# Third layer of a four-layer network on one Trainium2 core: VectorE's scans, statistics and last additions moved behind the multiplications of the first gates, denominators' sums one gate sooner

## The chip, the cores and the metric

The kernel runs on one core of a Trainium2 chip, in one launch. The metric is device time in microseconds. TensorE (PE) does the matrix products, VectorE (DVE), ScalarE (ACT) and GpSimd (POOL) the rest, SyncE (SP) issues the DMAs. Each engine has its own queue and works it off in order. An instruction that waits for a semaphore holds up all that stands behind it on its engine.

## The reference

Four layers run one after the other on x of 4 × 512 × 256 floats. Each is `x = x + attention(layernorm(x)) + feedforward(layernorm(x))`. The change touches only the third:

```
# attention: linear, with a decayed running sum over the tokens
q, k, v = split(xn @ w_qkv);  q, k = elu(q) + 1, elu(k) + 1      # 16 heads of 16
kvsum[t] = decay * kvsum[t-1] + k[t] * v[t]
ksum[t]  = decay * ksum[t-1] + k[t]
den = clip(sum over the head of q * ksum, 1e-6)
attention = (q * kvsum / den) @ w_out
# feedforward: weights rounded to -1, 0, 1 times a scale of their group
gate, up = split(xn @ ternary(w_gate_up).T)                      # 1024 each
h = silu(gate) * up
feedforward = (h / sqrt(mean(h * h) + eps)) @ ternary(w_proj).T
```

## The kernel before

The third layer is `layer2`. It goes through the batch's four elements b, one after the other, in a pipeline. All five engines have their code written out in one order each, and semaphores alone tie them together. Nothing plans the order at run time. Tiles are 128 channels × 512 tokens; x stays in tiles of 128 tokens × 256 channels.

What TensorE does for an element: eight pairs of gate and up products (`gates(b, j)`, j = 0 to 7, L1816, eight matmuls each, since the input is split into two halves of 16 bits, `xhi` and `xlo`); behind pair 3 the sums over heads for the denominators (`denominators`, L1828); behind pair 5 the turning of their reciprocals (`turn_denominators`, L1839); behind pair 7 the spreading of the reciprocals over the channels (`spread_denominators`, L1847). Then come the turning of the next element's normalised input (`turn_input`, L1791), the attention's projection (`project_attention`, L1853), the next element's q, k and v (`queries_keys_values`, L1803), this one's second feedforward product (`project_gated`, L1865), and the sums of squares for its norm (`sum_squares`, L1878). Pair j waits for h of pair j-2, since both use the same two banks.

For pair j, ScalarE computes silu (L1662), VectorE multiplies (h, L1746), ScalarE rounds h to 16 bits (`hhi`, L1647) and squares it (L1650), VectorE takes the rest (`hlo`, L1714, in `rest_of_gated`), and GpSimd adds the square to a running sum (L1612, `add_square`).

Beside that, in the order before:
- VectorE's four scans of an element (`sum_up`, L1708 and L1709) stand behind its products k·v and ahead of its first h. GpSimd makes `qk` (L1605) and `num` (L1606) from them, and one semaphore, `qprod`, tells that both are done.
- The layer norm of the next element: its statistics (`norm_stats`, L100 to L106) stand between h of pairs 0 and 1, then GpSimd's power (L1594, `invert`), then VectorE's `shifts` (L1688) behind pair 1, then ScalarE's `normalise` (L1633, four activations) behind silu, rounding and squaring of pair 3.
- VectorE's clip and reciprocal of the denominators (L1759, L1761) stand behind pair 4, `attnT` (L1764) behind pair 7.
- At the end of an element VectorE scales its norm (L1724), GpSimd takes the power (L1624), and VectorE adds the four tiles of the second product to x (L1732, `add_projected`).
- In the first three elements a slice of the next layer's weights is made ternary (`TernaryMeans`).
- Behind the last element TensorE runs three products whose result nobody reads (`keep_going`, L113).

Of the kernel before, what the change touches and what calls it, by code (L numbers as in the profile page):

```python
# [1491 lines left out]
def layer2(k):  # L1492
# [4 lines left out]
    with ExitStack() as ctx:  # L1497
# [48 lines left out]
        scanned = sem("scanned")  # L1546
        qprod = sem("qprod")
        den_made = sem("den_made")
        rden_ready = sem("rden_ready")
# [23 lines left out]
        Z_ORDER = [(2, 0), (3, 1), (0, 2), (1, 3), (4, 6), (5, 7)]  # L1573
        DEN_AT, RT_AT, SPREAD_AT = 3, 5, 7
        means = TernaryMeans(k, sb, sem)
        block = ctx.enter_context(nc.Block())

# [11 lines left out]
        def _(pool):  # L1589
# [12 lines left out]
            def weigh_queries(b):  # L1602
                pool.wait_ge(scanned, b * CT + CT)
                pool.wait_ge(feat_ready, b * 4 + 4)
                nc.gpsimd.tensor_tensor(qk[:, :, :], feat[:, 0:CT, :], ksum[:, :, :], ALU.mult)  # L1605
                nc.gpsimd.tensor_tensor(num[:, :, :], feat[:, 0:CT, :], kvsum[:, :, :], ALU.mult).then_inc(qprod, 1)  # L1606

# [8 lines left out]
            for b in range(B):  # L1616
                weigh_queries(b)
                invert(b + 1)
                for j in range(1, HT):
                    add_square(b, j)  # L1620
                if b + 1 < B:
                    split_input(b + 1)
                pool.wait_ge(ss_ready, b + 1)
                nc.gpsimd.tensor_tensor(inv[:, :], inv[:, :], k.minus_half[:, 0:TT], ALU.pow).then_inc(inv_ready, 1)  # L1624

        @block.scalar
        def _(act):
# [29 lines left out]
            for b in range(B):  # L1657
                for j in range(HT):
# [6 lines left out]
                    if j == RT_AT + 1:  # L1665
                        act.wait_ge(rt_made, b + 1)
                        nc.scalar.activation(rdenT[:, :], ps[7][0:L2_HEADS, :], ACT.Copy).then_inc(rt_ready, 1)
                    if j == 3:
                        normalise(b + 1)
# [8 lines left out]
        def _(dve):  # L1678
            own = Own(dve, dve_own)

            def statistics(b):
                if b == B:
                    dve.wait_ge(x_done, TT)
                norm_stats(k, dve, own, lambda t: k.x[:, b % B, t, :], stats, mv, rstd, var_ready)

# [13 lines left out]

            def sum_up(b):  # L1700
                dve.wait_ge(feat_ready, b * 4 + 2)
                for c in range(CT):
                    dve.wait_ge(z_made, b * 6 + (4 + c + 1))
                    nc.vector.tensor_tensor(kv[:, c, :], feat[:, 2 + c, :], ps[V_BANK[c]][:, :], ALU.mult).then_inc(kv_ready, 1)
                for c in range(CT):
                    dve.wait_ge(kv_ready, b * CT + (c + 1))
                    rate = decay[:, c:c + 1].broadcast_to([P, S])
                    nc.vector.tensor_tensor_scan(ksum[:, c, :], rate, feat[:, 2 + c, :], 0.0, ALU.mult, ALU.add)  # L1708
                    nc.vector.tensor_tensor_scan(kvsum[:, c, :], rate, kv[:, c, :], 0.0, ALU.mult,  # L1709
                                                 ALU.add).then_inc(scanned, 1)  # L1710
# [11 lines left out]
            def norm_gated(b):  # L1722
                dve.wait_ge(ss_made, b + 1)
                nc.vector.tensor_scalar(inv[:, :], ps[6][:, 0:TT], 1.0 / HID, float(np.finfo(np.float32).eps),  # L1724
                                        ALU.mult, ALU.add).then_inc(ss_ready, 1)

            def add_projected(b):
                dve.wait_ge(inv_ready, b + 1)
                dve.wait_ge(aout_added, b * 2 + 2)
                for t in range(TT):  # L1730
                    dve.wait_ge(fout_made, b * 2 + (t // 2 + 1))
# [5 lines left out]
            features(0)  # L1737
            sum_up(0)
            for b in range(B):
                for j in range(HT):  # L1740
# [7 lines left out]
                    if j:  # L1748
                        rest_of_gated(b, j - 1)
                    if j == 0:  # L1750
                        statistics(b + 1)
                    if j == 1:
                        shifts(b + 1)
                    if j == DEN_AT + 1:
                        dve.wait_ge(den_made, b + 1)
                        if b < means.SLICES:
# [3 lines left out]
                                                         1e-6, None, ALU.max))  # L1760
                        nc.vector.reciprocal(rden[:, :, :], rden[:, :, :]).then_inc(rden_ready, 1)  # L1761
                for c in range(CT):
                    dve.wait_ge(spread, b * CT + (c + 1))
# [9 lines left out]
                if b + 1 < B:  # L1773
                    features(b + 1)
                    sum_up(b + 1)
                norm_gated(b)
                add_projected(b)

        @block.tensor
        def _(pe):  # L1780
# [90 lines left out]
            def sum_squares(b):  # L1871
# [3 lines left out]
                else:  # L1875
                    pe.wait_ge(aout_added, b * 2 + 2)
                for t in range(TT):
                    last = nc.tensor.matmul(ps[6][:, t:t + 1], sqsum[:, t * P:(t + 1) * P], k.ones[:, 0:1], start=True, stop=True)  # L1878
                last.then_inc(ss_made, 1)
# [5 lines left out]
            for b in range(B):  # L1885
                pe.wait_ge(split, b + 1)
                for j in range(HT):
                    gates(b, j)
                    if j == DEN_AT:
                        denominators(b)  # L1890
# [7 lines left out]
                if b + 1 < B:  # L1898
                    queries_keys_values(b + 1)
                project_gated(b)  # L1900
                sum_squares(b)
            keep_going(k, ps[0][:, :], w.qkv[:, 0, 0:S], 3)
# [909 lines left out]
```

## Time and profile before

| | |
|---|---|
| time, median of 3 runs | 1026.82 us (1026.48 to 1027.84) |
| time of the profiled execution | 1027.12 us |
| its span | 1025.3 us, mean granted clock of TensorE 0.973 |
| busy over the whole span | PE 945.7 us (92%), DVE 714.5 (70%), ACT 464.9 (45%), POOL 434.6 (42%) |
| third layer, TensorE's first and last instruction | 441.36 us to 624.7 us |
| first gate pair of the four elements | 454.07, 503.03, 546.29, 589.56 us |

Times in the rows are microseconds from the start of the span. A row of the timeline reads: start, duration, engine, line and operation, what is written and what is read, count, and in brackets the engine's idle time just before it with what released it. Instructions on one engine overlap: a duration reaches from start to the end of the last write, so the next can start earlier.

### The profile page before, as it was taken

The page shows a single profiled execution, that of the slowest core. Times are in us where ns is not written, and L with a number is a line of the kernel's source. Part 1 is how long each engine was busy: PE and PEld are TensorE (multiplying, and loading weights), DVE is VectorE, ACT ScalarE, POOL GpSimd, SP SyncE. Part 2 cuts the span into 40 slices and gives each one's busy share as a digit, 9 for nine tenths or more (in the row PEclk, how much of TensorE's full clock was granted, in tenths as well). Part 3 has the DMA queues.
Part 4 walks back from the last instruction along what each step waited for, and adds up shares of the span by engine and source line. Part 5 has one row for each costly group of instructions (what it writes and reads, how often), then busy time and mean ns, then how long its engine had stood idle before and what let it go on. Part 6 is the DMA issues. An engine that isn't in the chain of part 4 may idle for free. (4 is left out here: it accounts for less than half of the span.)

```text
span 1025.3 us, 12736 instructions
## 1 busy us (share of the span) xinstructions
PE 945.7 (92%) x4562; PEld 488.2 (48%) x4566; DVE 714.5 (70%) x1311; ACT 464.9 (45%) x767; POOL 434.6 (42%) x444
## 2 busy tenths in 40 slices
PE   8999887889999999878999998999999999999997
PEld 5677554423333333344555645623752464265324
DVE  3677564578888878557777773767686687759673
ACT  3333154247766666755575462612461345125311
POOL 2222456454444334026344361186138406830860
PEclk9999999779999999999999998999999999999999
DMA  9600044312211220030000001000000000000000
GB/s 315 241 16 16 16 141 113 107 47 68 62 48 51 63 63 2 1 146 1 16 16 1 17 0 44 1 1 1 21 1 1 1 21 0 1 1 22 1 1 21
DMA packets 28958, 43.68 MB, mean 43 GB/s; under 512 B 6528, under 2 KB 22096, under 8 KB 28496
## 3 DMA queue, kind: packets, MB, share of 16 engines
q1 hardware_dynamic: 28896, 42.87, 13.4%
q8 instruction: 37, 0.61, 0.2%
q14 instruction: 25, 0.20, 0.1%
HBM read 31.38 MB, written 11.27 MB: 42 GB/s over the span
## 5 line engine op out<-in xcount | busy, mean ns | idle before, releaser
L2214 POOL TENSOR_TENSOR l_scaled<-l_X,l_source 128x512 f32<-128x512 f32 x112 | 135.6, 1240 | 141.1 <-ACT l_X L2284 124.0
L1134 DVE TENSOR_REDUCE l_nmax<-banks 128x1 f32<-128x512 f32 (+1 forms) x165 | 147.9, 929 | 35.1 <-PE banks L1243 34.2
L1089 ACT ACTIVATE l1b_PT<-banks 128x512 f32<-128x512 f32 (+1 forms) x176 | 134.1, 793 | 67.0 <-PE banks L1256 66.7
L1243 PE MATMUL banks<-l_KQ 96*128 96x512 bf16 x240 | 81.8, 394 | 8.0 <-DVE l_nmax L1134 5.2
L1256 PE MATMUL banks<-l_KQ 99*128 99x512 bf16 x256 | 85.6, 388 | 3.1 <-ACT l1b_PT L1089 2.1
L2297 ACT ACTIVATE l_hhi<-l_h 128x512 f16<-128x512 f32 (+1 forms) x24 | 15.1, 630 | 129.4 <-DVE l_h L2409 129.4
L2633 PE MATMUL banks<-l_scaled,l_cbm 128*64 128x512 f32 x224 | 59.5, 613 | 10.7 <-POOL l_scaled L2214 9.2
L1270 PE MATMUL banks<-l1b_PT,l1b_V 128*32 128x512 f32 x512 | 68.2, 605 | 0.0
L2383 DVE TENSOR_TENSOR l_decayed<-banks,l_right_decay 128x512 f32<-128x512 f32 x56 | 38.4, 686 | 37.9 <-PE banks L2633 37.9
L2655 PE MATMUL banks<-l_decayed,w_place 64*128 64x512 f32 x224 | 63.2, 641 | 0.0
L1816 PE MATMUL banks<-l_xhi,l_ternary 128*128 128x512 f16 x128 | 49.3, 385 | 9.0 <-DVE l_h L1746 9.0
L2322 DVE SCALAR_TENSOR_TENSOR l_conv<-l_padded,w_taps,l_conv 128x512 f32<-128x512 f32 x72 | 52.5, 750 | 3.2 <-ACT l_conv L2273 1.5
L1256 PEld LDWEIGHTS banks<-l_KQ 99*128 99x128 bf16 x256 | 22.3, 101 | 64.3 <-ACT l1b_PT L1089 47.5
L1612 POOL TENSOR_TENSOR l_sqsum<-l_sqsum,l_sq 128x512 f32<-128x512 f32 x28 | 40.4, 1444 | 23.7 <-ACT l_sq L1650 22.5
L1816 PE MATMUL banks<-l_xlo,l_ternary 128*128 128x512 f16 x128 | 49.4, 386 | 0.0
L2555 PE MATMUL banks<-l_xnT,w_inner 128*128 128x512 f32 x96 | 44.0, 616 | 0.0
L1803 PE MATMUL banks<-l_xnT,w_qkv 128*128 128x512 f32 x96 | 41.9, 593 | 1.3 <-DVE l_xnT L1692 1.3
L1243 PEld LDWEIGHTS banks<-l_KQ 96*128 96x128 bf16 x240 | 22.8, 99 | 40.0 <-DVE l_nmax L1134 14.8
L1054 POOL TENSOR_SCALAR l1b_above<-l1b_gate,l1b_trial 128x256 f32<-128x256 f32 x45 | 40.9, 922 | 1.6 <-DMA l1b_gate<-l_gate 1.6
L2525 PE MATMUL banks<-l_xhi,l_up 128*128 128x512 f16 (+1 forms) x96 | 36.5, 380 | 0.0
L2525 PE MATMUL banks<-l_xlo,l_up 128*128 128x512 f16 (+1 forms) x96 | 36.4, 379 | 0.0
L2633 PEld LDWEIGHTS banks<-l_scaled,l_cbm 128*64 128x64 f32 x224 | 12.1, 135 | 49.7 <-DVE l_decayed L2383 27.4
(346 smaller groups left out, 2073.8 us busy)
## 6 DMA issues: line engine op xcount, KB each, us to landing
l_split<-l1a_parts SPq DMA_DIRECT2D x16, 384.0 KB, 3.4
l_KQ<-l_split SPq DMA_DIRECT2D x48, 128.0 KB, 2.8
l_KQ<-l_split SPq DMA_DIRECT2D x16, 192.0 KB, 3.1
l_KQ<-l_split SPq DMA_DIRECT2D x48, 64.0 KB, 2.8
w_ternary<-l_tern_out SPq DMA_DIRECT2D x7, 384.0 KB, 2.3
l_raw<-in_w_gate_up SPq DMA_DIRECT2D x2, 1024.0 KB, 9.8
out<-x SPq DMA_DIRECT2D x4, 512.0 KB, 3.3
w_qkv<-in_w_qkv SPq DMA_DIRECT2D x2, 768.0 KB, 5.9
```

Source lines behind the costliest of these rows:

```text
L1089: nc.scalar.activation(PT[:, first:first + size, :], source, ACT.Exp, scale=SCALE).then_inc(p_ready, 1)
L1134: nc.vector.tensor_reduce(nmax[:, H % 2, first:first + size], source, axis=AX.X, op=ALU.max, negate=True).then_inc(smax_read, 1)
L1243: last = nc.tensor.matmul(ps[bank + m][:, :], KQ[pairs, QUERY, g, j, t * P:(t + 1) * P], KQ[pairs, KEY, g, j, :], start=True, stop=True)
L1256: last = nc.tensor.matmul(ps[KEY_BANK + bank + m][:, :], KQ[whole, KEY, g, j, kt * P:(kt + 1) * P], KQ[whole, QUERY, g, j, :], start=True, ...
L1270: last = nc.tensor.matmul(ps[OUT_BANK][j * LANE:(j + 1) * LANE, :], V[:, kt, g * LANES + j, :], PT[:, kt * LANES + j, :], start=(kt == 0), ...
L1816: last = nc.tensor.matmul(ps[2 * (j % 2) + part][:, :], gate_up[:, c, first:first + P], x[:, c, :], start=(c == 0 and x is xhi), stop=(c = ...
L2214: nc.gpsimd.tensor_tensor(by_head(scaled[:, (2 * u + m) % 4, :]), by_head(X[:, T, :]), spread(source[:, level, T, :]), ALU.mult).then_inc( ...
L2322: last = nc.vector.scalar_tensor_tensor(conv[:, n, :], padded[:, n % PADS, tap:tap + S], w.taps[:, n, tap:tap + 1], conv[:, n, :], ALU.mul ...
L2525: last = nc.tensor.matmul(ps[2 * (j % 2) + u][0:rows, :], w.up[:, u, c, j * P:j * P + rows], x[:, c, :], start=(c == 0 and x is xhi), stop ...
L2555: last = nc.tensor.matmul(ps[CHANNEL_BANK[n]][:, :], w.inner[:, c, X0 + n * P:X0 + (n + 1) * P], xnT[:, c, :], start=(c == 0), stop=(c == ...
L2633: last = nc.tensor.matmul(bank[rows, :], cbm[:, 2 * pair + m, level, :], scaled[:, (2 * u + m) % 4, :], start=True, stop=True, tile_positi ...
L2655: last = nc.tensor.matmul(ps[6 + m][:, :], w.place[rows, level, :], decayed[rows, u % 3, :], start=(level == 0), stop=(level == LEVELS - 1))
```

## The change

In the first element, VectorE's scans move behind h of pair 0 (channel tile 0) and behind h and hlo of pair 1 (channel tile 1). In the other three, the four additions of the element before move from its end to the same two places. Statistics of the next element move to pairs 2 and 3, their aggregation (now `variance`) to pair 4, `shifts` to pair 5, and ScalarE's `normalise` from pair 3 to pair 6. GpSimd's power for it moves from ahead of the squares' additions to behind the third. `qk` and `num` get a semaphore each, so that the denominators' sums wait for `qk` alone; they stand behind pair 2 in place of 3 in the last three elements, and the reciprocals behind pair 3 in place of 4. In the last element the sums of squares go to another bank and stand ahead of the second product.

```
-        DEN_AT, RT_AT, SPREAD_AT = 3, 5, 7
+        DEN_AT, RT_AT, SPREAD_AT = (3, 2, 2, 2), 5, 7
+        STATISTICS_AT = (2, 2, 2, 2)
+        def squares_bank(b):
+            return 6 if b + 1 < B else 2
 # GpSimd
-                nc.gpsimd.tensor_tensor(qk[:, :, :], feat[:, 0:CT, :], ksum[:, :, :], ALU.mult)
-                nc.gpsimd.tensor_tensor(num[:, :, :], feat[:, 0:CT, :], kvsum[:, :, :], ALU.mult).then_inc(qprod, 1)
+                nc.gpsimd.tensor_tensor(qk[:, :, :], feat[:, 0:CT, :], ksum[:, :, :], ALU.mult).then_inc(qprod, 1)
+                nc.gpsimd.tensor_tensor(num[:, :, :], feat[:, 0:CT, :], kvsum[:, :, :], ALU.mult).then_inc(num_ready, 1)
...
-                invert(b + 1)
                 for j in range(1, HT):
                     add_square(b, j)
+                    if j == STATISTICS_AT[b] + 1:
+                        invert(b + 1)
 # ScalarE
-                    if j == 3:
+                    if j == STATISTICS_AT[b] + 4:
                         normalise(b + 1)
 # VectorE
-            sum_up(0)
+            keys_times_values(0)
...
-                    if j == 0:
-                        statistics(b + 1)
-                    if j == 1:
+                    if j < CT and b == 0:
+                        scan(b, (j,))
+                    elif j < CT:
+                        add_projected(b - 1, (2 * j, 2 * j + 1))
+                    if j - STATISTICS_AT[b] in (0, 1):
+                        first = 2 * (j - STATISTICS_AT[b])
+                        statistics(b + 1, (first, first + 1))
+                    if j == STATISTICS_AT[b] + 2:
+                        variance()
+                    if j == STATISTICS_AT[b] + 3:
                         shifts(b + 1)
-                    if j == DEN_AT + 1:
+                    if j == DEN_AT[b] + 1:
...
-                    sum_up(b + 1)
+                    keys_times_values(b + 1)
+                    scan(b + 1, range(CT))
                 norm_gated(b)
-                add_projected(b)
+            add_projected(B - 1, range(TT))
 # TensorE
-                    pe.wait_ge(aout_added, b * 2 + 2)
+                    pe.wait_ge(h_ready, B * HT)
...
-                    if j == DEN_AT:
+                    if j == DEN_AT[b]:
...
-                project_gated(b)
-                sum_squares(b)
+                    project_gated(b)
+                    sum_squares(b)
+                else:
+                    sum_squares(b)
+                    project_gated(b)
```

VectorE in the first element before the change, from the products k·v (`l_kv`) to h of pair 3, as the program has them:

```order
L1704 TENSOR_TENSOR l_kv<-l_feat,banks 128x512 x2
L1708 SCALAR_TENSOR_TENSOR l_ksum<-l_decay,l_feat 128x512
L1709 SCALAR_TENSOR_TENSOR l_kvsum<-l_decay,l_kv 128x512
L1708 SCALAR_TENSOR_TENSOR l_ksum<-l_decay,l_feat 128x512
L1709 SCALAR_TENSOR_TENSOR l_kvsum<-l_decay,l_kv 128x512
L1746 TENSOR_TENSOR l_h<-l_act_gate,banks 128x512
L100 BN_STATS l_stats<-x 128x6 x4
L104 BN_AGGR l_mv<-l_stats 128x2 x4
L106 TENSOR_SCALAR l_rstd<-l_mv 128x4
L1746 TENSOR_TENSOR l_h<-l_act_gate,banks 128x512
L1714 TENSOR_TENSOR l_hlo<-l_h,l_hhi 128x512
```

The same engine and place with the change:

```order
L1720 TENSOR_TENSOR l_kv<-l_feat,banks 128x512 x2
L1764 TENSOR_TENSOR l_h<-l_act_gate,banks 128x512
L1726 SCALAR_TENSOR_TENSOR l_ksum<-l_decay,l_feat 128x512
L1727 SCALAR_TENSOR_TENSOR l_kvsum<-l_decay,l_kv 128x512
L1764 TENSOR_TENSOR l_h<-l_act_gate,banks 128x512
L1732 TENSOR_TENSOR l_hlo<-l_h,l_hhi 128x512
L1726 SCALAR_TENSOR_TENSOR l_ksum<-l_decay,l_feat 128x512
L1727 SCALAR_TENSOR_TENSOR l_kvsum<-l_decay,l_kv 128x512
L1764 TENSOR_TENSOR l_h<-l_act_gate,banks 128x512
L1732 TENSOR_TENSOR l_hlo<-l_h,l_hhi 128x512
L1692 BN_STATS l_stats<-x 128x6 x2
```

h of pair 0 now has no scan ahead of it, and h of pairs 1 and 2 have two each; the statistics have gone behind pair 2. (L1720, L1764, L1726, L1732 of the changed program are L1704, L1746, L1708, L1714 of the one before.)

ScalarE in the first element with the change, from silu of pair 6 to its last squares; before, the row of four (`x<-x,l_shift,l_rstd`, `normalise`) stands three pairs earlier:

```order
L1669 ACTIVATE l_act_gate<-banks 128x512
L1654 ACTIVATE l_hhi<-l_h 128x512
L1657 ACTIVATE l_sq<-l_h 128x512
L1674 ACTIVATE l_rdenT<-banks 16x512
L1640 ACTIVATE x<-x,l_shift,l_rstd 128x256 x4
L1669 ACTIVATE l_act_gate<-banks 128x512
L1654 ACTIVATE l_hhi<-l_h 128x512
L1657 ACTIVATE l_sq<-l_h 128x512
```

The four activations now stand between silu of pair 6 and silu of pair 7 (the second L1669), in every element.

## Rows read from the trace of the kernel before

**Rows 1.** Waits, third layer: engine and instruction <- releaser: us, times, longest

```profile
PE banks L1816 <- DVE l_h L1746: 9.0, 8, 2.9
PE banks L1839 <- DVE l_rden L1761: 2.9, 4, 0.8
PE banks L1853 <- DVE l_attnT L1764: 0.8, 1, 0.8
```

**Rows 2.** Timeline of TensorE, first element

```profile
460.07 0.39 PE L1816 MATMUL banks<-l_xhi,l_ternary 128*128 128x512 f16 x1 [2.39 <-DVE l_h L1746]
...
464.85 0.39 PE L1816 MATMUL banks<-l_xhi,l_ternary 128*128 128x512 f16 x1 [2.88 <-DVE l_h L1746]
...
466.28 0.63 PE L1816 MATMUL banks<-l_xhi,l_ternary 128*128 128x512 f16 x1
...
467.99 2.12 PE L1828 MATMUL banks<-w_select,l_qk 128*128 128x8 f32 x16
...
474.63 0.60 PE L1839 MATMUL banks<-ident,l_rden 128*16 128x128 f32 x4 [0.83 <-DVE l_rden L1761]
...
481.45 3.64 PE L1853 MATMUL banks<-w_out,l_attnT 128*128 128x256 f32 x16
```

**Rows 3.** Windows: stretch, us, busy of each engine, granted clock, DMA

```profile
466.00:470.00 4.00, 4.00 (x23) 2.81 (x21) 2.40 (x4) 3.48 (x7) 3.03 (x2) 0.68 0.00 0
```

**Rows 4.** Timeline of the other engines, first element

```profile
456.39 1.09 ACT L1662 ACTIVATE l_act_gate<-banks 128x512 f32<-128x512 f32 x2
...
461.84 2.33 POOL L1606 TENSOR_TENSOR l_num<-l_feat,l_kvsum 128x1024 f32<-128x1024 f32 x1
461.85 2.35 DVE L106 TENSOR_SCALAR l_rstd<-l_mv 128x4 f32<-128x4 f32 x1
...
476.13 0.60 ACT L1662 ACTIVATE l_act_gate<-banks 128x512 f32<-128x512 f32 x1 [1.52 <-PE banks L1816]
...
477.67 0.57 ACT L1667 ACTIVATE l_rdenT<-banks 16x512 f32<-16x512 f32 x1
478.14 0.57 ACT L1662 ACTIVATE l_act_gate<-banks 128x512 f32<-128x512 f32 x1
...
479.99 1.33 DVE L1764 TENSOR_TENSOR l_attnT<-l_num,banks 128x512 f32<-128x512 f32 x2
```

**Rows 5.** Groups of instructions, third layer: count, busy us, mean ns, idle before

```profile
L1708 DVE TENSOR_TENSOR_SCAN l_ksum<-l_decay,l_feat 128x512 f32<-128x512 f32 x8 | 9.7, 1207 | 0.0
...
L1633 ACT ACTIVATE x<-x,l_shift,l_rstd 128x256 f32<-128x256 f32 x16 | 8.3, 588 | 0.0
```

**Rows 6.** Timeline, VectorE and GpSimd, second element, behind pair 4

```profile
518.29 1.51 DVE L1714 TENSOR_TENSOR l_hlo<-l_h,l_hhi 128x512 f16<-128x512 f32 x1
...
517.99 1.27 POOL L1612 TENSOR_TENSOR l_sqsum<-l_sqsum,l_sq 128x512 f32<-128x512 f32 x1
```

**Rows 7.** Timeline of TensorE and ScalarE, second element

```profile
503.03 0.38 PE L1816 MATMUL banks<-l_xhi,l_ternary 128*128 128x512 f16 x1
503.25 0.38 PE L1816 MATMUL banks<-l_xlo,l_ternary 128*128 128x512 f16 x1
...
511.53 1.85 PE L1828 MATMUL banks<-w_select,l_qk 128*128 128x8 f32 x16
...
524.71 3.64 PE L1853 MATMUL banks<-w_out,l_attnT 128*128 128x256 f32 x16
...
521.40 0.57 ACT L1662 ACTIVATE l_act_gate<-banks 128x512 f32<-128x512 f32 x1
```

**Rows 8.** Timeline, last element and the layer's end

```profile
589.56 0.38 PE L1816 MATMUL banks<-l_xhi,l_ternary 128*128 128x512 f16 x1
...
610.55 3.72 PE L1853 MATMUL banks<-w_out,l_attnT 128*128 128x256 f32 x16 [0.78 <-DVE l_attnT L1764]
...
621.91 2.82 PE L113 MATMUL banks<-w_qkv,ident 128*128 128x512 f32 x6
...
623.38 1.66 DVE L1732 SCALAR_TENSOR_TENSOR x<-banks,l_inv,x 128x256 f32<-128x256 f32 x4 [1.13 <-POOL l_inv L1624]
```

More of the change, by code:

```diff
@@ L1547, in layer2 @@
         qprod = sem("qprod")
+        num_ready = sem("num_ready")
         den_made = sem("den_made")
@@ L1679, in _, with statistics, variance @@
             own = Own(dve, dve_own)
-            def statistics(b):
+            def statistics(b, tiles):
                 if b == B:
                     dve.wait_ge(x_done, TT)
-                norm_stats(k, dve, own, lambda t: k.x[:, b % B, t, :], stats, mv, rstd, var_ready)
+                for t in tiles:
+                    own.note(nc.vector.bn_stats(stats[:, t, :], k.x[:, b % B, t, :]))
+            def variance():
+                own.settle()
+                dve.nop(nofuse=True)
+                for t in range(TT):
+                    last = nc.vector.bn_aggr(mv[:, t, :], stats[:, t, :])
+                own.link(last)
+                nc.vector.tensor_scalar(rstd[:, :], mv[:, :, 1], LN_EPS, None, ALU.add).then_inc(var_ready, 1)
             def shifts(b):
@@ L1698, in features, with keys_times_values @@
                                                    ALU.add).then_inc(feat_ready, 1)
-            def sum_up(b):
+            def keys_times_values(b):
                 dve.wait_ge(feat_ready, b * 4 + 2)
@@ L1704, in sum_up, with scan @@
                     nc.vector.tensor_tensor(kv[:, c, :], feat[:, 2 + c, :], ps[V_BANK[c]][:, :], ALU.mult).then_inc(kv_ready, 1)
-                for c in range(CT):
+            def scan(b, channels):
+                for c in channels:
                     dve.wait_ge(kv_ready, b * CT + (c + 1))
@@ L1723, in norm_gated, with add_projected @@
                 dve.wait_ge(ss_made, b + 1)
-                nc.vector.tensor_scalar(inv[:, :], ps[6][:, 0:TT], 1.0 / HID, float(np.finfo(np.float32).eps),
+                nc.vector.tensor_scalar(inv[:, :], ps[squares_bank(b)][:, 0:TT], 1.0 / HID, float(np.finfo(np.float32).eps),
                                         ALU.mult, ALU.add).then_inc(ss_ready, 1)
-            def add_projected(b):
+            def add_projected(b, tiles):
                 dve.wait_ge(inv_ready, b + 1)
                 dve.wait_ge(aout_added, b * 2 + 2)
-                for t in range(TT):
+                for t in tiles:
                     dve.wait_ge(fout_made, b * 2 + (t // 2 + 1))
@@ L1761, in _ @@
                         nc.vector.reciprocal(rden[:, :, :], rden[:, :, :]).then_inc(rden_ready, 1)
+                dve.wait_ge(num_ready, b + 1)
                 for c in range(CT):
@@ L1875, in sum_squares @@
                 else:
-                    pe.wait_ge(aout_added, b * 2 + 2)
+                    pe.wait_ge(h_ready, B * HT)
                 for t in range(TT):
-                    last = nc.tensor.matmul(ps[6][:, t:t + 1], sqsum[:, t * P:(t + 1) * P], k.ones[:, 0:1], start=True, stop=True)
+                    last = nc.tensor.matmul(ps[squares_bank(b)][:, t:t + 1], sqsum[:, t * P:(t + 1) * P], k.ones[:, 0:1], start=True, stop=True)
                 last.then_inc(ss_made, 1)
```

## The prediction, made before the changed kernel ran

> **What bounds the kernel now.** I read the waits of the third layer first: they say what could be gained at all. TensorE stands 9.0 us for h in eight waits, 2.9 us for the reciprocals of the denominators in four, and 0.8 us for `attnT` in one [rows 1]. That is 12.7 us in all, and nothing else of the layer is touched. Then I read TensorE's timeline of each element for where these waits lie. The first element has 2.39 us ahead of pair 2 and 2.88 us ahead of pair 3, because its first h stands behind four scans and its second behind the statistics [rows 2]. The other three share what is left of the 9.0 us: (9.0 - 2.39 - 2.88) / 3 = 1.24 us each. Behind the two long waits TensorE's granted clock falls to 0.68 in a stretch of 4 us, so to its level of 1.2 GHz in most of it, and a matmul of 512 columns takes 0.63 us in place of 0.39 [rows 2, 3]. Last come the timelines of ScalarE and VectorE, since the edits also put work later on these two: the question is what stands there when TensorE no longer waits early.
>
> **First element, the early part.** I follow the instructions by their durations. Silu of pair 0 is done by 457.0 (two silus from 456.39, 1.09 us together) [rows 4], so h of pair 0 is done at 457.7 and pair 2 starts then, 2.3 us before its 460.07. A pair takes 8 × 0.216 = 1.73 us, from the two starts of 503.03 and 503.25 [rows 7]. Two scans of 1.2 us [rows 5] follow and overlap a little: h of pair 1 is done at 460.55. Pair 3 starts at 460.6, against 464.85 [rows 2]: 4.2 us gained. Two more scans end at 463.4, and only then can GpSimd make `qk`. I take for it the 2.33 us of `num`, which is of the same size [rows 4]: done at 465.8. Pair 3 was done at 462.4, so TensorE stands 3.5 us for `qk`, where it did not stand before. The sums start at 465.85 and not at 467.99 [rows 2]: of 4.2 us, 2.1 are left.
>
> **First element, the reciprocals.** VectorE's `hlo` of pair 1 is asked for at 464.0 and GpSimd reads at that time. In rows 6 an `hlo` takes 1.51 us where a GpSimd addition of 1.27 us began 0.30 us before it; it ends some 0.54 us behind that addition. L106 took 2.35 us, with its end at that of `num`, which had started 0.01 us before it [rows 4]. So this `hlo` ends at 466.35, h of pair 3 at 467.6, the next `hlo` waits for `num` (466.2 to 468.6) and ends at 469.1, and after two statistics h of pair 4 is done at 470.4. Then in order: `hlo` of pair 3 (behind an addition, up to 1 us more), four aggregations and L106 (behind another, 0.6 us), then clip and reciprocal. By the same durations this gives 474.4 for the transposes, which started at 474.63 [rows 2]. Everything gained before is gone here but 0.2 us. TensorE has finished pair 5 at 471.2 and waits 3.2 us.
>
> **First element, the late part.** Before, silu of pair 6 starts at 476.13, its rounding and square follow, the copy `rdenT` at 477.67 and silu of pair 7 at 478.14. `attnT` then starts at 479.99, takes 1.33 us, and is done at 481.32, just ahead of the projection at 481.45 [rows 2, 4]. Now `normalise` stands between the copy and silu of pair 7: four activations of 0.59 us, overlapped 8.3 / 4 = 2.06 us by their group's busy time, at least 1.96 us until the next can start [rows 5]. Less the 0.2 us, silu of pair 7 comes at 479.9 and `attnT` is done at 483.05. TensorE, which before went without a wait from the transposes at 474.63 to the projection at 481.45, is ready at 474.4 + 6.8 = 481.2 [rows 2] and waits 1.9 us. The projection starts at 483.1: 1.6 us later than before. The first element costs +1.6 us.
>
> **Elements two and three.** Times from pair 0. Pairs 0 to 2 run without a wait (5.2), the sums with the total 1.9 [rows 7], pairs 3 to 5 another 5.2, the transposes 0.4: pair 6 can start at 12.9 if the reciprocals are there. Its silu starts at 14.0, the rounding waits 0.2 us for h of pair 5, and the chain rounding, square, copy, `normalise` takes 0.5 + 0.5 + 0.5 + 2.0 us: silu of pair 7 at 18.2. Before it was 521.40 - 503.03 = 18.37 [rows 7]. `attnT` ends at 21.4, the projection starts at 21.45 against 524.71 - 503.03 = 21.68 [rows 7]. All of the 2.07 us that TensorE stood early (1.24 for h, 0.8 for the reciprocals) turns up as about 2.1 us in front of the projection. Gain 0.2 us each, -0.4 us for both. The additions moved behind h of pairs 0 and 1 come before nothing that TensorE waits for: h of pair 2 has 0.8 us to spare.
>
> **Last element.** There is no turning of an input (about 1 us of cover), and the reciprocals come 0.8 us after pair 5, because `hlo` of pair 2 finds GpSimd in its second addition. The same chain puts the projection 21.9 us behind pair 0, against 610.55 - 589.56 = 20.99 [rows 8]: +0.9 us. At the end, the sums of squares leave the path to the last additions, some 2 us shorter on VectorE. But `keep_going` still stands behind the second product and ends at 621.91 + 2.82 = 624.73, and the last addition ended at 623.38 + 1.66 = 625.04 [rows 8]. So no more than 0.3 us comes of it.
>
> **The clock.** The trace shows the low level once here, behind 5.3 us of waits within 7 us [rows 2, 3]. Now there are waits of 3.5 and 3.2 us in the first element. If the clock falls again the sums or pair 4 lose 0.3 to 0.6 us ahead of the reciprocals, while pairs 6 and 7 are hidden behind `normalise`. Bounds 0 and 1; I take 0.3.
>
> The Trainium skill (TensorE: Matmul & The Clock Gate, What's actually happening) says that an idle TensorE falls to half its clock and busy work brings it back. The trace agrees: 0.68 behind the two waits [rows 3]. By that rule the fall comes again, and the sum would be at the upper end of this term.
>
> **Sum.** 1.6 - 0.4 + 0.9 - 0.3 + 0.3 = +2.1 us. On the profiled execution's own 1027.12 us (span 1025.3, 1.8 us around it) that is 1029.2; this execution stands 0.3 us over the median of the runs, 1026.82. Forecast 1028.9 us.
>
> **Rivals.**
> A, slower still: in elements two and three `hlo` of pair 2 is asked for at 9.83 us from pair 0, and GpSimd's second addition at 9.87, when the square is there. Whichever is first holds the other up. If GpSimd is, `hlo` ends 1.1 us later, with it the statistics, the reciprocals, pairs 6 and 7 and the chain behind. Twice 1.1 is +2.2 us: 1031.1. For it: 0.04 us decides, and L106 lost by 0.01 us [rows 4]. Against it: by my times VectorE is first. Were I to misjudge the same meeting in the first element to the kernel's favour (`hlo` of pair 3 against an addition), it would give 0.9 us back.
> The Trainium skill (SBUF — State Buffer, Who interferes with whom) says that a VectorE instruction with two inputs in SBUF and a GpSimd one that reads it shut each other out, first come first served, for the whole instruction. The trace agrees with 1.51 us for an `hlo` [rows 6]. It speaks against this change, as it puts the scans' readers on GpSimd beside the first `hlo`s.
> B, faster: `normalise` finds a hole on ScalarE, or silu of pair 7 is early enough. Then the waits of rows 1 really go: about 2 us in each of elements two to four and 0.3 at the end, less the first element's loss, some -5 us: 1022. For it: 12.7 us of waits. Against it: in-order ScalarE has `normalise` ahead of silu of pair 7 in every element, with 4.1 us of work from silu of pair 6 to silu of pair 7, where TensorE needs 1.7 for a pair. It decides when the group at L1633 ends before pair 7's gate is there.
> C, no difference: losses of the first and last element come out at half, about +0.8: 1027.6. For it: the first element's meeting with the port goes VectorE's way, and the clock doesn't fall. That would also be the outcome if TensorE's early gain were exactly returned in all four.
>
> **How the numbers follow.** Forecast 0.48 (its own range 1028.0 to 1029.9), A 0.24, B 0.12, C 0.16. Runs of this kernel differ by over a us, so 0.2% (2.05 us) is about what can be told from no change; the forecast stands right on that bound, 1028.87. I put 0.27 of its 0.48 above it, the rest below. Slower: 0.27 + 0.24 = 0.51. Same: 0.21 + 0.16 = 0.37. Faster: 0.12. The range leaves out the lower part of B and little of A: 1026.3 to 1031.6.
>
> **What would show it.** In the changed profile: `normalise` right ahead of the last silu, and TensorE's wait for `attnT` (L1853 before) grown from 0.8 us in one to about 9 us in four; the waits for h down to 2 to 3 us, all but little in the first element; a new wait of about 3.5 us for `qk` and one of about 3 us for the reciprocals in the first element; the distance from the second to the third element's pair 0 at 43.0 against 43.26 us, or 44.1 with rival A. I am wrong if the wait for `attnT` stays under 3 us in all, or if the first element is shorter than its 48.96 us (454.07 to 503.03).

## The result, and the profile after

The changed kernel takes 1037.7 us (median of 6 runs, 1033.59 to 1040.04) against 1026.88 us (6 runs, 1025.65 to 1027.84): 10.8 us slower, a ratio of 1.010 with a 95% interval of 1.0077 to 1.0122. The forecast, 1028.9 us, had the sign; its range ended at 1031.6. The profiled execution took 1038.54 us (span 1036.7, mean granted clock 0.962; before 1027.12, 1025.3 and 0.973).

| stage (profiled executions) | before, us | after, us | difference |
|---|---|---|---|
| start to the layer's first turning of x | 441.36 | 444.20 | +2.84 |
| from there to the first element's pair 0 | 12.71 | 14.41 | +1.70 |
| first element, pair 0 to pair 0 | 48.96 | 52.56 | +3.60 |
| second | 43.26 | 46.31 | +3.05 |
| third | 43.27 | 45.02 | +1.75 |
| last pair 0 to the next layer's first product | 36.73 | 38.69 | +1.96 |
| the rest | 399.0 | 395.5 | -3.5 |

The first and the last row have the same code on both sides. They differ by where TensorE's clock happened to be low (47.8 against 41.0 us ahead of the layer, 2.7 against 10.7 behind it), and nearly cancel. The layer itself has the other 12.06 us. Of these the 1.70 us ahead of pair 0 are a low stretch too, from 446.9 to 450.4 us, in the products for q, k and v, whose code on TensorE the change leaves as it was. In several of the kernels below such a stretch lies at the layer's start, in others not. So 10.36 us are left for the change.

The waits of TensorE in the third layer, after (engine and instruction <- releaser: us, times, longest), against [rows 1]:

```profile
PE banks L1880 <- DVE l_attnT L1790: 8.5, 4, 3.0
PE banks L1855 <- POOL l_qk L1611: 3.4, 1, 3.4
...
PE banks L1866 <- DVE l_rden L1786: 1.6, 2, 0.9
...
PE banks L1843 <- DVE l_h L1764: 0.2, 1, 0.2
```

Before 12.7 us, now 13.7. What was spread over eight waits for h, two of them long, is now one wait of 1.6 to 3.0 us in each element, in front of the projection. TensorE's timeline shows what stands there and behind it; `w_out` rows are the projection, the first rows answer to [rows 2], the last two to [rows 7, 8]:

```profile
469.45 2.53 PE L1855 MATMUL banks<-w_select,l_qk 128*128 128x8 f32 x16 [3.38 <-POOL l_qk L1611]
...
479.36 0.60 PE L1866 MATMUL banks<-ident,l_rden 128*16 128x128 f32 x4 [0.92 <-DVE l_rden L1786]
...
487.98 5.25 PE L1880 MATMUL banks<-w_out,l_attnT 128*128 128x256 f32 x16 [1.63 <-DVE l_attnT L1790]
...
532.84 6.70 PE L1880 MATMUL banks<-w_out,l_attnT 128*128 128x256 f32 x16 [1.90 <-DVE l_attnT L1790]
...
624.59 5.21 PE L1880 MATMUL banks<-w_out,l_attnT 128*128 128x256 f32 x16 [3.05 <-DVE l_attnT L1790]
```

The sixteen matmuls of the projection took 3.64 us before [rows 2, 7] and take 5.2 to 6.7 us now. They didn't change; the clock did. Windows of after (stretch, us, busy time of PE, PEld, DVE, ACT, POOL, granted clock, DMA share, GB/s):

```profile
442.00:454.00 12.00, 8.63 (x23) 4.12 (x23) 2.23 (x4) 5.79 (x9) 3.72 (x4) 0.86 0.71 272
...
470.00:478.00 8.00, 8.00 (x30) 4.38 (x30) 5.42 (x12) 2.05 (x4) 6.36 (x4) 0.57 0.00 0
487.00:496.00 9.00, 8.02 (x23) 5.57 (x24) 6.20 (x9) 1.96 (x4) 5.70 (x4) 0.81 0.01 2
532.00:542.00 10.00, 9.16 (x23) 6.45 (x24) 5.79 (x8) 1.52 (x4) 5.56 (x4) 0.66 0.00 0
579.00:588.00 9.00, 8.84 (x25) 6.01 (x26) 6.05 (x8) 1.81 (x3) 4.88 (x4) 0.81 0.00 0
624.00:632.00 8.00, 7.41 (x39) 6.43 (x40) 2.67 (x5) 0.10 (x1) 3.14 (x3) 0.79 0.01 2
```

And the same view of before, at the layer's start, the first element's waits and two projections:

```profile
439.00:451.00 12.00, 8.64 (x27) 4.19 (x26) 3.21 (x5) 6.88 (x11) 3.73 (x4) 1.00 0.71 271
462.00:474.00 12.00, 8.96 (x42) 4.97 (x42) 8.20 (x13) 7.40 (x15) 7.25 (x5) 0.86 0.00 0
...
481.00:490.00 9.00, 9.00 (x34) 5.80 (x33) 6.93 (x9) 3.69 (x6) 5.05 (x4) 1.00 0.02 7
524.00:533.00 9.00, 9.00 (x36) 5.96 (x35) 6.94 (x9) 3.51 (x6) 5.31 (x4) 1.00 0.00 0
```

A window at clock c was at the low level, 1.2 GHz, for (1 - c) / 0.5 of its length. For the row 470:478 that is 0.86 × 8 = 6.9 us. The six rows give 3.4 + 6.9 + 3.4 + 6.8 + 3.4 + 3.4 = 27 us, against 3.4 us before. Where TensorE has work all the time, work at half clock takes twice as long, so at most half of the 24 us more is lost, 12 us. That this is close to the 12.06 us of the layer is chance: the waits cost something too. It is less than 12 us, because some of the low stretches lies under waits that were there anyway. How much less, e2 shows below.

Why the projection waits is on ScalarE, second element of after, against 521.40 in [rows 7]:

```profile
525.09 0.60 ACT L1669 ACTIVATE l_act_gate<-banks 128x512 f32<-128x512 f32 x1
525.96 0.63 ACT L1654 ACTIVATE l_hhi<-l_h 128x512 f16<-128x512 f32 x1 [0.28 <-DVE l_h L1764]
526.50 0.61 ACT L1657 ACTIVATE l_sq<-l_h 128x512 f32<-128x512 f32 x1
527.02 0.57 ACT L1674 ACTIVATE l_rdenT<-banks 16x512 f32<-16x512 f32 x1
527.72 2.08 ACT L1640 ACTIVATE x<-x,l_shift,l_rstd 128x256 f32<-128x256 f32 x4
529.70 0.57 ACT L1669 ACTIVATE l_act_gate<-banks 128x512 f32<-128x512 f32 x1
```

`normalise` (L1640) stands right ahead of the last silu (L1669), as forecast. From silu of pair 6 to silu of pair 7 it is 4.6 us; 4.2 was forecast. VectorE's `attnT` starts at 531.51 and lasts 1.28 us, and the projection starts at 532.84, 21.67 us behind its pair 0 (before 21.68).

### The profile page after: what moved, and what is told of

Same layout as the page of the kernel before. It is cut to its first block and busy times, and to the rows that moved or that the text cites. A ratio compares the mean times of both kernels' runs of the same rounds, so it can differ in the third digit from the quotient of the medians.

```text
span 1036.7 us, 12743 instructions
## 1 busy us (share of the span) xinstructions
PE 957.7 (92%) x4562; PEld 496.0 (48%) x4566; DVE 718.8 (69%) x1311; ACT 465.3 (45%) x767; POOL 433.9 (42%) x444
## 5 line engine op out<-in xcount | busy, mean ns | idle before, releaser
L2663 PE MATMUL banks<-l_scaled,l_cbm 128*64 128x512 f32 x224 | 59.5, 613 | 10.7 <-POOL l_scaled L2244 10.6
L1669 ACT ACTIVATE l_act_gate<-banks 128x512 f32<-128x512 f32 x32 | 19.0, 594 | 46.0 <-PE banks L1843 45.1
```

What stands on the lines that cost most here:

```text
L2663: last = nc.tensor.matmul(bank[rows, :], cbm[:, 2 * pair + m, level, :], scaled[:, (2 * u + m) % 4, :], start=True, stop=True, tile_positi ...
```

## The experiments

The theory after the result: the waits themselves cost what was forecast, about 2 us; the other some 9 us are TensorE's clock, which falls behind each wait ahead of the projection. The rivals: the time is lost on the engines' own chains (reciprocals, port), with the clock a bystander; or it comes from the scans and the wait for `qk`. Before was run again beside each group of experiments, and each ratio is against its own: medians 1026.75 (e1 to e4), 1027.47 (e5 to e8) and 1028.33 us (e9 to e11), 29 runs each.

**`normalise` alone (e1).** The kernel before, with one number changed.

```
-                    if j == 3:
+                    if j == 6:
                         normalise(b + 1)
```

> The kernel before with one edit: ScalarE's normalise stands behind pair 6 in place of pair 3, nothing else moves. Theory N+C (normalise makes attnT late, and each such wait brings TensorE's clock down for 3.4 to 6.8 us at half speed right behind it): the waits for attnT in front of L1853 go from 0.8 us in one element to about 9 us in four (2.0, 2.0, 2.0, 2.9), +7.6 us by these alone, and low-clock stretches appear behind most of them, another 1.7 us for each 3.4 us: +12 to +16 us, 1039 to 1043 us. Rival N (the waits cost only themselves, the clock in the changed kernel fell for another reason, the scans' and reciprocals' waits of the first element): +7 to +8 us, 1034 to 1035. Rival P (normalise is not what makes attnT late): no difference within 1 us.

Measured: 1043.21 us, ratio 1.0153 (1.0121 to 1.0185), 16.5 us slower than before. It is more than the whole change costs. The waits for h and the reciprocals are as in [rows 1], 9.0 and 2.9 us; the one ahead of the projection is new, and the clock is low behind all four:

```profile
PE banks L1853 <- DVE l_attnT L1764: 7.6, 4, 2.7
```

```profile
480.00:489.00 9.00, 8.14 (x21) 5.96 (x22) 5.00 (x8) 0.85 (x2) 5.58 (x4) 0.64 0.01 2
528.00:538.00 10.00, 9.22 (x23) 6.42 (x24) 6.02 (x9) 1.78 (x4) 5.50 (x4) 0.68 0.00 0
575.00:585.00 10.00, 8.36 (x22) 5.96 (x22) 6.09 (x9) 1.84 (x5) 6.17 (x4) 0.66 0.00 0
623.00:633.00 10.00, 9.16 (x41) 7.49 (x42) 2.77 (x5) 0.35 (x1) 2.37 (x2) 0.66 0.01 2
```

**The wait filled (e2).** The changed kernel, with products that nobody reads ahead of the projection. They don't shorten the chain to `attnT`; they only keep TensorE at work.

```
+                keep_going(k, ps[6][:, :], w.qkv[:, 0, 0:S], 3 if b + 1 == B else 2)
                 project_attention(b)
```

> The changed kernel, and TensorE runs products whose result is overwritten (two of 128x512 in fp32, three in the last element, 0.86 us each, into bank 6) ahead of the attention's projection, where it waits for attnT (1.6, 1.9, 1.9, 3.05 us). Theory C (the clock falls because TensorE is idle there, and this is where 10 us of the 10.8 come from): the granted clock stays high behind these places in all four elements, TensorE's order and waits otherwise the same; the layer loses four or five low stretches of 3.4 us, so 5 to 8 us faster than the changed kernel, 1029.5 to 1032.5. Rival (the time is lost by the waits' chain through ScalarE and VectorE itself, low clock hidden beside it): same as the changed kernel, 1036 to 1039, or slower by the products.

Measured: 1027.7 us (12 runs), ratio 1.0008 (0.9989 to 1.0027) against before. The ratio of the change was 1.010, so added work takes away (1.010 - 1.0008) × 1026.8 = 9.4 us, with an uncertainty of about 3 us from the two intervals. The same stretches of e2:

```profile
481.00:490.00 9.00, 9.00 (x30) 5.40 (x29) 7.74 (x10) 3.48 (x6) 6.14 (x4) 1.00 0.01 2
525.00:535.00 10.00, 9.81 (x32) 5.74 (x31) 7.93 (x11) 4.45 (x8) 5.47 (x4) 1.00 0.07 28
569.00:578.00 9.00, 8.91 (x29) 5.62 (x30) 7.20 (x9) 3.46 (x6) 4.84 (x3) 1.00 0.04 17
612.00:620.00 8.00, 7.72 (x52) 6.47 (x51) 2.92 (x6) 0.34 (x1) 3.39 (x3) 1.00 0.01 2
```

In the second element the projection starts 21.67 us behind pair 0, just as in the changed kernel: what comes ahead of it is no faster, only what stands behind it. The profiled executions agree with the medians. From pair 0 to pair 0, and from the last to the next layer, after loses 2.02, 2.98, 1.68 and 1.50 us against e2, 8.2 us in all, with 20.5 us more at the low level. The remaining 2.2 of the 10.36 us are what e2 loses against before. So this kernel is also the changed one without the clock's part behind the projections, and it tests the other terms (below). Its waits:

```profile
PE banks L1855 <- POOL l_qk L1611: 3.4, 1, 3.4
PE banks L1866 <- DVE l_rden L1786: 2.8, 2, 2.1
...
PE banks L1880 <- DVE l_attnT L1790: 0.7, 3, 0.3
```

**Half filled (e5).** As e2 with one product less each time (`2 if b + 1 == B else 1`).

> The kernel of e2 with one overwritten product less at each place: one ahead of the projection in elements one to three (0.86 us of a wait of 1.9), two in the last (1.7 of 3.05), so TensorE still stands about 1 us and 1.3 us there. Theory C with a threshold (a stand of 1.2 us did not bring the clock down in the kernel before, one of 1.9 did in every element): the clock stays high in most elements, time as e2, 1027 to 1030 us. Rival (any stand behind the spreading and the turning, which keep TensorE little busy, brings it down): low stretches come back behind the projections, 1034 to 1038 us.

Measured: 1027.92 us, ratio 1.0015 (0.9992 to 1.0038). TensorE waits again, and the clock stays up; here the wait, and the second element's projection:

```profile
PE banks L1880 <- DVE l_attnT L1790: 4.0, 4, 1.1
```

```profile
531.00:541.00 10.00, 8.96 (x29) 5.43 (x29) 8.38 (x11) 4.45 (x8) 6.18 (x4) 1.00 0.00 0
```

So in this execution four waits of 0.8 to 1.1 us ahead of the projection cost next to nothing. In the changed kernel, at 1.6 to 3.0 us, the clock fell behind all four. That is no threshold: in other kernels it fell behind 0.8 and 1.0 us too (last section).

**`normalise` alone, filled (e9).** e1 with the products of e2.

> The kernel of e1 (before, with normalise behind pair 6 alone) with the overwritten products of e2 ahead of the attention's projection. It parts the 16.4 us of e1 into the wait and the clock. Theory N+C: the waits for attnT stay as a place (the products fill them), 7.6 us of loss remain, less what the earlier first pairs give nothing; the low stretches behind the projections are gone: 1034 to 1035.5 us. Rival (the clock is worth less than half of it): 1038 to 1042.

Measured: 1032.02 us, ratio 1.0041 (1.0013 to 1.0069); of its 12 executions one took 2421 us, which leaves the median as it is. Of e1's 1.53% the clock is 1.1%, some 11.5 us (give or take 4); windows of 10 us from 480, 526, 571 and 616 us are all at 1.00. The other 4.2 us are the wait itself (interval 1.3 to 7.1; 7.6 were expected), since here the waits for h stay too. The trace has 45.14 us from pair 0 to pair 0, against 43.26, and 1.9 us more in the last element as well. The first is only 0.2 us longer, since before has its low stretch there and e9 has none. That makes 5.8 us in the four.

**Statistics two gates sooner (e3).** The changed kernel, with `normalise` behind the square of pair 4 in place of 6.

```
-        STATISTICS_AT = (2, 2, 2, 2)
+        STATISTICS_AT = (0, 0, 0, 0)
```

> The changed kernel with the statistics of the next element at pairs 0 and 1, variance behind pair 2, shifts behind pair 3 and normalise behind pair 4 (all two pairs earlier; the rest of the change stays). Theory N+C: normalise is out of the way of silu of pair 7, the waits for attnT fall to under 0.3 us in elements one to three and about 1 us in the last; following the instructions by the durations of the trace of before, pair-0-to-pair-0 distance of elements two and three is 41.9 us (before 43.26), with no fall of the clock behind the projections: 8 to 12 us faster than the changed kernel, 1026 to 1029, as the first element still has its 3.5 us wait for qk. Rival (the change costs by the additions behind h of pairs 0 and 1, or by the sums one pair sooner): stays above 1034.

Measured: 1031.55 us, ratio 1.0025 (1.0003 to 1.0048). The wait ahead of the projection is gone but for 1.0 us, once. The other three waits on VectorE's work grow:

```profile
PE banks L1866 <- DVE l_rden L1786: 4.9, 4, 2.4
...
PE banks L1843 <- DVE l_h L1764: 1.7, 2, 1.6
...
PE banks L1874 <- ACT l_rdenT L1674: 1.1, 3, 0.4
```

Elements two and three take 42.56 and 42.90 us, 0.4 to 0.7 less than before. The first (63.31 us from the first turning to the second pair 0, before 61.67) and the last (37.68, before 36.73) lose more; in the last the clock fell for 3.4 us at the projection, behind the wait of 1.0 us. The gain that was expected of the shorter chain (41.9 us for elements two and three, no fall of the clock) is there in small part only.

**One gate later (e6).** `STATISTICS_AT[b] + 5` in place of + 4 for `normalise`, which puts it behind the last silu.

> The changed kernel with normalise one pair later on ScalarE, behind silu, rounding and squaring of pair 7. By following the durations, attnT comes in time in elements one to three, and in its place TensorE stands 1.4 to 1.6 us for the normalised input ahead of the turning (L1818), and about 2 us for attnT in the last element. Theory C: the place of the wait does not matter, its length does: with 1.5 us some of the three lose the clock, with 2 us the last does: 1030 to 1036 us. Rival (only ScalarE's chain counts): 0.5 us per element less than the changed kernel, 1036 us.

Measured: 1034.29 us, ratio 1.006 (1.0036 to 1.0084). The wait has moved to the next reader of ScalarE's work, the turning of x. There the clock falls too, behind the two waits of 1.7 us and not behind the one of 1.2 us:

```profile
PE banks L1818 <- ACT x L1640: 4.5, 3, 1.7
...
PE banks L1880 <- DVE l_attnT L1790: 2.8, 1, 2.8
```

```profile
528.00:538.00 10.00, 9.51 (x33) 6.92 (x34) 6.76 (x10) 3.59 (x6) 4.76 (x3) 0.83 0.00 0
```

**Scans back (e4).** The changed kernel, with the first element's scans again ahead of its first h.

```
             keys_times_values(0)
+            scan(0, range(CT))
...
-                    if j < CT and b == 0:
-                        scan(b, (j,))
-                    elif j < CT:
+                    if j < CT and b:
                         add_projected(b - 1, (2 * j, 2 * j + 1))
```

> The changed kernel, with the first element's four scans ahead of its first h again as before. Theory: this undoes the wait for qk (3.4 us) and leaves that for attnT (1.6 to 3 us in all four). The first element is 3 to 4 us shorter than in the changed kernel, less one low-clock stretch: 4 to 5 us faster, 1033 us, and elements two to four are unchanged. Rival (the first element's late part is bound by normalise alone): under 1 us, 1037.

Measured: 1031.59 us, but from 1026.64 us at a clock of 0.972 to 1038.52 at 0.962; ratio 1.0045 (1.0018 to 1.0071). The wait for `qk` is gone, and 2.4 us for h are back in its place. The wait ahead of the projection is the same 8.5 us in four. The profiled execution is the slowest one and as long as the changed kernel's, 1036.7 us of span. So in some executions the clock seems to let these same waits pass. That is read from the mean granted clock; no trace of a faster execution was kept.

**Both (e8).** e4 with e3's statistics.

> A version meant to beat both: the changed kernel with the statistics two pairs earlier as in e3, and the first element's scans ahead of its first h as in e4. Theory: no wait for qk, none for attnT in three elements, no fall of the clock behind projections; the waits for h in elements two to four stay away. The distance of pair 0 to pair 0 42.6 to 42.9 us (measured in e3) against 43.26, the first element 1 to 3 us shorter than before: 1022 to 1026 us against 1026.8. Rival (what the statistics' new place costs on VectorE eats it): 1026 to 1029.

Measured: 1026.43 us, ratio 0.9989 (0.9969 to 1.0009): no difference from before. The waits of TensorE on the layer's own work are 7.9 us, against 12.7 [rows 1]:

```profile
PE banks L1865 <- DVE l_rden L1785: 3.3, 4, 1.0
PE banks L1842 <- DVE l_h L1765: 2.5, 2, 2.4
...
PE banks L1873 <- ACT l_rdenT L1674: 1.1, 3, 0.4
PE banks L1879 <- DVE l_attnT L1789: 1.0, 1, 1.0
```

What the shorter waits bring is partly given back. From the first pair 0 to the next layer it is 170.7 us in the trace, against 172.2, with three low stretches of 3.4 us against one: behind the wait for h in the first element, at the third projection with no wait of over 1.0 us near (the row below), and at the last projection, behind 1.0 us:

```profile
566.00:575.00 9.00, 9.00 (x30) 6.23 (x29) 5.98 (x8) 1.95 (x4) 5.32 (x4) 0.81 0.00 0
```

**The end alone (e7, e11).** The kernel before with only the last element's sums of squares in bank 2 and ahead of the second product. It ran once as e7 and twelve times as e11.

> The kernel before, with the last element's part alone: sums of squares into another bank and ahead of the second product. Theory (keep_going ends the layer): last addition some 2 us after the last matmul of the second product in place of about 4, but the next layer's first product comes only 0.3 us sooner; from the last element's pair 0 to it 36.4 us against 36.73. Rival (the additions were what ended the layer): 2 us sooner, 34.7.

> The kernel of e7 again, timed: the last element's part alone on the kernel before. One profile gave 36.08 us from the last pair 0 to the next layer against 36.73, 0.65 us less. Theory: 0.5 to 0.7 us faster than before, which the spread of these runs hides: 1026 to 1027. Rival (its one time of 1023.8 was not luck): 2 us or more faster.

Measured: 1023.79 us once; then 1025.57 us in 12 runs, ratio 0.9973 (0.9948 to 0.9998). From the last pair 0 to the next layer it is 36.08 us (before 36.73), and the idle time at the handover is 1.00 us (before 1.56). In the second profile it is 37.77 us, with 3.4 us of low clock in it; less the half, it is 36.07 again. So a gain of 0.65 us is seen in the traces, more than the 0.3 that the prediction gave the end; that the median gained 2.8 isn't explained by it.

**Both, with products in the waits (e10).** e8 with two products that nobody reads ahead of pair 2 of the first element, one ahead of each turning of the reciprocals, and one ahead of the last projection.

```
+                    if b == 0 and j == 2:
+                        pe.wait_ge(kv_ready, CT)
+                        keep_going(k, ps[6][:, :], w.qkv[:, 0, 0:S], 2)
                     gates(b, j)
...
                     if j == RT_AT:
+                        if b:
+                            pe.wait_ge(x_done, b * TT)
+                        keep_going(k, ps[4][:, :], w.qkv[:, 0, 0:S], 1)
                         turn_denominators(b)
...
                 if b + 1 < B:
                     turn_input(b + 1)
+                else:
+                    keep_going(k, ps[6][:, :], w.qkv[:, 0, 0:S], 1)
                 project_attention(b)
```

> The kernel of e8 with overwritten products where TensorE still stands: two of 128x512 in fp32 ahead of pair 2 of the first element (a wait of 2.4 us), one ahead of the transposes of the reciprocals in each element (waits of 0.7 to 1.0 us), one ahead of the last projection (1.0 us). Theory C: the low stretches that e8 still had (at 464, 567 and 611 us of its span) become rare, 1.7 us each; the products cost under 0.3 us: 1022 to 1025 us against 1026.4 of e8. Rival (the clock falls behind the spreading and the turning whatever stands there): no difference from e8.

Measured: 1022.15 us (12 runs), ratio 0.994 (0.9915 to 0.9965): faster than both kernels. Waits on the layer's own work are down to 3.8 us:

```profile
PE banks L1865 <- DVE l_rden L1785: 1.9, 1, 1.9
PE banks L1873 <- ACT l_rdenT L1674: 1.1, 3, 0.4
...
PE banks L1842 <- DVE l_h L1765: 0.8, 2, 0.7
```

That low stretches would become rare was wrong: at the projections of elements two to four the clock still falls, 0.83, 0.81 and 0.81 in windows of 9 or 10 us. And the trace doesn't show where the gain comes from. From the first pair 0 to the next layer it has 172.4 us, as before (172.2), though its execution took 1023.27 us against 1027.12. That e10 is faster is measured; why is not shown.

## Why the prediction was wrong

The step that failed is the clock's term: "Bounds 0 and 1; I take 0.3". I looked for the fall only where the row of before had it, in the first element, and priced only that. The new waits ahead of the projections, which I had myself put at about 9 us in four, got no clock term, though they are nearly as long as the two waits of the first element behind which the row shows 0.68 [rows 3]. Measured, the term is 9.4 us by e2's median and 8.2 us by its trace. In the rows of after the four falls last 3.4, 6.8, 3.4 and 3.4 us, 17 us at half clock, which is 8.5 us. With 9.4 in place of 0.3 the sum would have given 1038.0, against 1037.7 measured.

The Trainium skill (TensorE: Matmul & The Clock Gate, HAM oscillation — how this bites in real kernels) describes a kernel in which a wait in each pass of a loop brings the low level back in each pass; its waits are for a DMA and last 3 to 5 us. The traces agree, with shorter waits: four of 1.6 to 3.0 us, four windows of 0.66 to 0.81.

The other terms, read from e2, where the clock is up behind the projections:
- *First element, +1.6.* In e2 it takes 504.07 - 453.53 = 50.54 us, +1.58. The wait for `qk` is 3.4 us (forecast 3.5). The reciprocals' is 2.1 us (3.2), and the transposes start 20.26 us behind pair 0 (20.33). In after itself that wait is only 0.9 us, because TensorE was at half clock in pairs 4 and 5 (0.57 in 470:478) and came late to it. The total is right in part by luck, since two steps on the way were off. The sums start 10.84 us behind pair 0, not 11.78. I took silu of pair 0 from the row of before, 2.3 us behind pair 0 [rows 4]; it starts 1.06 us behind it in e2 and in after. In before ScalarE had been held by a transfer of the next layer's weights:

```profile
453.50 1.48 ACT L2020 ACTIVATE l_hi<-l_raw 128x1536 bf16<-128x1536 f32 x1 [1.41 <-DMA l_raw<-in_w_down]
```

  The 0.9 us were then lost again: the clock was low for 3.4 us behind the wait for `qk` in e2 as well, and TensorE came to the end of pair 5 about 1 us later than I had it, under a wait that was there anyway.
- *Elements two and three, -0.4.* 43.33 and 43.34 us against 43.26 and 43.27: +0.1. The order of the chain was right (projection at 21.67 us in after, 21.45 forecast), so the 0.2 us that each should have gained is missing.
- *Last element, +0.9 and -0.3.* 37.19 against 36.73: +0.5, forecast +0.6. In after the projection comes 22.09 us behind pair 0, forecast 21.9; the end by itself gains 0.65 (e7), not 0.3.
- These sum to +2.2 us with the clock up behind the projections, against +1.8 forecast.
- *`attnT` wait of about 9 us in four:* 8.5 in four. *h down to 2 to 3 us:* 0.2 in after, 0.2 in e2. Pairs 2 to 4 of the first element found their h in time, but for 0.2 us ahead of pair 3.
- *Rival A* didn't occur: `hlo` of pair 2 in the second element starts at 520.97, GpSimd's addition at 521.05, and VectorE is first. *Rival B* did not occur, for the reason given. *Rival C* needed the clock to stay up. Its +0.8 is what e2's median shows (interval -1.1 to +2.8), so the times alone don't part it from the forecast's own +1.8; the trace of e2, with +2.2, speaks for the forecast.

The sign was right for the reason given, `normalise` ahead of the last silu: e1 shows that this edit alone costs 16.5 us. That e1 costs more than the whole change is settled in part. Some 3.4 us of it are the waits, since those for h stay (e9 has 4.2 us over before, e2 0.8). The rest is the clock: its falls are longer (windows of 0.64 to 0.68 in all four elements) behind waits no longer than those of after, and why is open. Also open is the difference between executions of one kernel: beside e9 to e11 before ran from 1024.4 to 1037.2 us, and e4 ranged over 12 us.

## What to carry to other kernels

A wait on TensorE has two prices: its length, and the half clock behind it. Where a reordering gathers waits into one in each pass (here 1.6 to 3.0 us), price the second for every pass, by a row of this kernel's at low clock, and say that it may or may not come. Products that nobody reads, put in the wait, are a cheap test of it, and here they also took the loss away. And before a step of an in-order engine is moved late, look at who reads the instruction right behind it.

## What the runs showed of the hardware

**Short waits and the clock.** Behind a wait of up to 1.1 us ahead of the projection the clock stayed up in four elements of e5. Behind 1.6, 1.9, 1.9 and 3.05 us in after it fell each time. But it also fell behind shorter ones. Here are the last projections of e11 and of e3; with the same wait of 0.78 us the one of before took 3.72 us [rows 8]:

```profile
610.01 5.41 PE L1857 MATMUL banks<-w_out,l_attnT 128*128 128x256 f32 x16 [0.78 <-DVE l_attnT L1768]
```

```profile
616.46 5.41 PE L1880 MATMUL banks<-w_out,l_attnT 128*128 128x256 f32 x16 [1.02 <-DVE l_attnT L1790]
```

Up to that point e11 has the code of before, so one program with one wait went both ways. In e10 the clock fell at the projections of elements two to four, where the only wait near is the one of 0.3 to 0.4 us for `rdenT`. So no length of a wait alone decides. What else does is open.

**A tiny VectorE instruction behind GpSimd.** In the changed kernel `shifts` (four columns) took 961 ns on average, 163 before. Here the group after, then before (count, busy us, mean ns, idle before):

```profile
L1704 DVE SCALAR_TENSOR_TENSOR l_shift<-l_mv,l_rstd 128x4 f32<-128x4 f32 x4 | 3.8, 961 | 0.0
```

```profile
L1688 DVE SCALAR_TENSOR_TENSOR l_shift<-l_mv,l_rstd 128x4 f32<-128x4 f32 x4 | 0.7, 163 | 0.0
```

In the second element of after, `shifts` started 0.15 us behind GpSimd's additions of squares:

```profile
526.45 1.23 DVE L1704 SCALAR_TENSOR_TENSOR l_shift<-l_mv,l_rstd 128x4 f32<-128x4 f32 x1
...
526.30 2.77 POOL L1618 TENSOR_TENSOR l_sqsum<-l_sqsum,l_sq 128x512 f32<-128x512 f32 x2
```

The first element's, with no addition begun just ahead, took 0.15 us at 481.03. So even a VectorE instruction of four columns can stand over 1 us beside GpSimd's. `normalise` waits for it, and its start at 527.72 is right behind the end at 527.68, some 0.2 us later than the copy ahead of it would have let it. In e2 the same instruction also takes 1.23 us in elements two and three, so this may be the 0.2 us that elements two and three didn't gain. That link is read from the traces and was not tried by a run.
